# Negating the imaginary query plane on ScalarE instead of VectorE, in a chunked complex linear-attention stage

## What is computed

```
c = (u @ W_qkva.T + b_qkva) as complex q, k, v, a   # 8 heads of 32
a = a * (rsqrt(|a|^2) * sigmoid(log |a|^2))
h_t = a_t * h_(t-1) + k_t (x) v_t        # (x): outer product, all complex
y_t = q_t . h_t
```

## Time and profile before

| | us |
|---|---|
| median of 3 runs | 3847.2 (3846.6 to 3855.82) |
| profiled execution, its time | 3847.57 |
| profiled execution, span of the records | 3845.7 |
| TensorE matmul busy | 2886.4 (75%) |
| VectorE busy | 2164.3 (56%) |
| ScalarE busy | 1078.8 (28%) |
| GpSimd busy | 653.4 (17%) |
| mean granted TensorE clock | 0.806 of full |
| share of the chain that ended last | PE 57%, DVE 21%, ACT 6%, POOL 5% |

### The profile page before, as it was taken

The page is one execution under the profiler, slowest core; times in us unless marked ns, Lnnn a source line. Parts: engine busy times, 40 slices in busy tenths (PEclk is TensorE's granted clock), DMA queues, the critical chain, the costliest instruction groups (busy, mean ns, idle before and its releaser), DMA issues.

```text
span 3845.7 us, 81835 instructions
## 1 busy us (share of the span) xinstructions
PE 2886.4 (75%) x35776; PEld 2163.0 (56%) x35776; DVE 2164.3 (56%) x4688; ACT 1078.8 (28%) x2076; POOL 653.4 (17%) x682
## 2 busy tenths in 40 slices
PE   4368669867986898499759866986688458999990
PEld 3244457445744664476447545744554447888880
DVE  4445776587659666956685677658544930101004
ACT  0212253124312522333243225312412322222220
POOL 0323300420060016002400420051001000000006
PEclk8577878877787878697868877887779678999995
DMA  2122201210121122012201220121100006565645
GB/s 80 23 56 51 45 2 47 71 29 17 42 71 18 40 46 55 8 40 57 45 7 40 61 45 2 51 67 24 40 23 33 2 21 215 191 193 193 200 152 175
DMA packets 230022, 247.56 MB, mean 64 GB/s; under 512 B 147360, under 2 KB 187168, under 8 KB 227360
## 3 DMA queue, kind: packets, MB, share of 16 engines
q1 hardware_dynamic: 223520, 225.54, 20.6%
q0 software_dynamic: 6144, 16.79, 1.4%
HBM read 196.15 MB, written 46.14 MB: 63 GB/s over the span
## 4 chain that ended last, share of the span: by engine, by line
PE 57%; DVE 21%; ACT 6%; POOL 5%; issue 4%; DMA 1%; SPq 0%; POOLq 0%; DVEq 0%
PE banks L1814 13%; PE banks L2316 7%; PE banks L2335 7%; PE banks L2047 4%; PE banks L2113 3%; POOL arena L1706 3%; PE banks L2128 2%; PE banks L1824 2%; PE banks L2133 2%; PE banks L1941 2%; POOL arena L1750 2%; PE banks L1946 2%; PE banks L1951 1%; PE banks L2069 1%; DVE arena L1468 1%
## 5 line engine op out<-in xcount | busy, mean ns | idle before, releaser
L1706 POOL TENSOR_TENSOR arena<-arena 128x1 f32<-128x1 f32 (+30 forms) x496 | 435.6, 909 | 607.1 <-DMA arena<-n_d 441.0
L2113 PE MATMUL banks<-arena 32*32 32x64 f32 (+2 forms) x6144 | 209.7, 327 | 215.8 <-DVE h_tok L1370 68.2
L1727 POOL DMA_INDIRECT h_d<-h_tok,pos_now x64 | 66.7, 1043 | 1707.4 <-DVE pos_now L1571 1690.3
L1149 DVE TENSOR_REDUCE arena<-arena 128x1 f32<-128x1 f32 (+30 forms) x496 | 243.7, 502 | 172.7 <-POOL arena L1706 168.3
L2113 PE MATMUL banks<-arena,xn 32*32 32x64 f32 (+2 forms) x6144 | 197.6, 330 | 181.7 <-DVE xn L1471 89.1
L2113 PEld LDWEIGHTS banks<-arena 32*32 32x32 f32 (+2 forms) x6144 | 191.4, 202 | 236.7 <-issue 144.8
L1814 PE MATMUL banks<-hT,ring 128*128 128x512 f32 x640 | 313.1, 642 | 8.7 <-DVE arena L1293 8.5
L2113 PEld LDWEIGHTS banks<-arena,xn 32*32 32x32 f32 (+2 forms) x6144 | 181.6, 198 | 196.1 <-issue 98.0
L881 ACT ACTIVATE arena<-banks 32x512 f32<-32x512 f32 x256 | 150.4, 588 | 455.0 <-DVE xn L1471 240.5
L2316 PE MATMUL banks<-arena 128*128 128x256 f32 x1248 | 276.7, 380 | 0.0
L2335 PE MATMUL banks<-arena 128*128 128x256 f32 x1248 | 275.7, 379 | 0.0
(11 more groups left out here) (337 smaller groups left out, 5247.3 us busy)
## 6 DMA issues: line engine op xcount, KB each, us to landing
arena<-in_w_ring SPq DMA_DIRECT2D x78, 1024.0 KB, 5.0
ring<-in_w_ring SPq DMA_DIRECT2D x104, 512.0 KB, 4.6
arena<-h_d SPq DMA_DIRECT2D x39, 256.0 KB, 5.3
y_d<-arena SPq DMA_DIRECT2D x39, 256.0 KB, 5.8
n_d<-NA SPq DMA_DIRECT2D x8, 1024.0 KB, 3.9
arena<-n_d SPq DMA_DIRECT2D x16, 512.0 KB, 7.5
u_d<-arena SPq DMA_DIRECT2D x8, 1024.0 KB, 3.8
NA<-u_d SPq DMA_DIRECT2D x32, 256.0 KB, 5.6
```

Of the source, the lines that this page charges most:

```text
L1149: dve.tensor_reduce(Usub[:, c, 0:t, t], part, AX.X, ALU.add).then_inc(*up(sub_sum, me))
L1706: pool.tensor_tensor(part, Usub[:, c, 0:t, 0:t], Nsub[:, c, t, 0:t].unsqueeze(1).to_broadcast([P, t, t]), ALU.mult)\
L2113: i_ = mm(bank[4 * hg + h][keys, b * width:(b + 1) * width], K2[rows_, r, b, keys], q, start=(r == 0), stop=(r == 1), skip_group_check=True)
```

## The change

ScalarE makes the negated plane everywhere, and VectorE no longer does. A semaphore `q_neg` marks the plane of the fresh queries (made by ScalarE after it has evicted them), `q_sum` is raised by VectorE's additions of the equal-token step and of every level, and `q_ready` is now raised by ScalarE, in a new function `turn_sign(k, hg)`. ScalarE's list becomes one loop over steps and groups: `turn_sign(k, hg)` first, then what the step has of `take_blocks`, or of `lay_near` and `lay_middle`. `lay_far` stays behind the loop. VectorE waits for `q_neg` ahead of line 1426 and for `q_ready` ahead of line 1454.

```diff
 # ScalarE, evicting the planes
+                            if c == 3:
+                                act.wait_ge(*at(plane_ok, n + 1))
+                                act.activation(Q3[:, 0], Q3[:, 2], ACT.Copy, scale=-1.0).then_inc(*up(q_neg, me))
 # ScalarE, steps
+                    def turn_sign(k, hg):
+
+                        act.wait_ge(*at(q_sum, 2 * k + hg + 1))
+                        Q3 = Q3s[hg]
+                        if k:
+                            halves = "p r b (n two m) -> p r (b n) two m"
+                            act.activation(Q3[:, 0:1].rearrange(halves, two=2, m=1 << (k - 1))[:, 0, :, 1],
+                                           Q3[:, 2:3].rearrange(halves, two=2, m=1 << (k - 1))[:, 0, :, 1], ACT.Copy,
+                                           scale=-1.0).then_inc(*up(q_ready, me))
+                        else:
+                            act.activation(Q3[:, 0], Q3[:, 2], ACT.Copy, scale=-1.0).then_inc(*up(q_ready, me))
...
-                    act.wait_ge(*at(q_ready, 3 * HG))
-                    act.wait_ge(*at(k_ready, HG))
-                    for k, hg in itertools.product(range(2, INNER + 1), range(HG)):
-                        take_blocks(k, hg)
-                    act.wait_ge(*at(zeroed, 6))
-                    for hg in range(HG):
-                        lay_near(hg)
-                    for hg in range(HG):
-                        lay_middle(hg)
+                    for k, hg in itertools.product(range(STEPS), range(HG)):
+                        turn_sign(k, hg)
+                        if k == 2 and hg == 0:
+                            act.wait_ge(*at(k_ready, HG))
+                        if 2 <= k <= INNER:
+                            take_blocks(k, hg)
+                        if k == INNER + 1:
+                            act.wait_ge(*at(zeroed, 6))
+                            lay_near(hg)
+                            lay_middle(hg)
                     for hg in range(HG):
                         lay_far(hg)
 # VectorE, fresh queries and equal-token step
-                        dve.wait_ge(*at(plane_ok, 6 * hg + 4))
-                        dve.tensor_scalar(Q3[:, 0], Q3[:, 2], -1.0, None, ALU.mult).then_inc(*up(q_ready, me))
...
+                        dve.wait_ge(*at(q_neg, hg + 1))
...
-                        step(dve.tensor_tensor(q2, t1[:, :, :], t2[:, :, :], ALU.add))
-                        dve.tensor_scalar(Q3[:, 0], Q3[:, 2], -1.0, None, ALU.mult).then_inc(*up(q_ready, me))
+                        dve.tensor_tensor(q2, t1[:, :, :], t2[:, :, :], ALU.add).then_inc(*up(q_sum, me))
 # VectorE, levels
+                        dve.wait_ge(*at(q_ready, 2 * lev + hg + 1))
...
-                        step(dve.tensor_tensor(q_hi, tmp(t1), tmp(t2), ALU.add))
-                        dve.tensor_scalar(q_lo[:, 0], q_hi[:, 1], -1.0, None, ALU.mult).then_inc(*up(q_ready, me))
+                        dve.tensor_tensor(q_hi, tmp(t1), tmp(t2), ALU.add).then_inc(*up(q_sum, me))
 # TensorE
-                        pe.wait_ge(*at(q_ready, 2 * k + hg + 1))
+                        pe.wait_ge(*(at(q_ready, 2 * (k - 1) + hg + 1) if k else at(q_neg, hg + 1)))
...
-                        pe.wait_ge(*at(q_ready, 2 * STEPS + hg + 1))
+                        pe.wait_ge(*at(q_ready, 2 * (STEPS - 1) + hg + 1))
```

More of the change, by code:

```diff
@@ L331, in build @@
         u_in = signal("u_in", nxt=64)
-        dve_step = signal("dve_step", rest=226, nxt=13, pre=36)
+        dve_step = signal("dve_step", rest=210, nxt=13, pre=36)
         pre_var = signal("pre_var", pre=1)
@@ L359, in build @@
         a_ok = signal("a_ok", rest=16)
-        q_ready = signal("q_ready", rest=18)
+        q_ready = signal("q_ready", rest=16)
+        q_neg = signal("q_neg", rest=2)
+        q_sum = signal("q_sum", rest=16)
         masked = signal("masked", rest=12)
@@ L987, in turn @@
                              kpT_ok, xx_ok, wt_ok, o_sq, ot_ok, exp_ok, sg_ok, u_ok, plane_ok, mag_root,
-                             hx_ok, block_ok, laid, laid_middle, y2_ok, kt_ok, y3_ok, h_tok_ok, rt_root, rt_exp])
+                             hx_ok, q_neg, q_ready, block_ok, laid, laid_middle, y2_ok, kt_ok, y3_ok, h_tok_ok, rt_root, rt_exp])
                 act.sem_inc(started.handle, 1)
@@ L1585, in turn @@
                              logit_sub, comb_ok, comb_copied, hid0_ok, x_done, mag_ok, v3_ok, a_ok,
-                             q_ready, masked, state_ok, hsq_ok, rt_var, rt_gap, hot_ok,
+                             q_sum, masked, state_ok, hsq_ok, rt_var, rt_gap, hot_ok,
                              pos_ok, k_ready])
```

## The result

| | before | after |
|---|---|---|
| median, us | 3846.9 (3842.8 to 3855.8, 4 runs) | 4086.0 (4079.6 to 4095.0, 4 runs) |
| profiled span, us | 3845.7 | 4085.1 |
| VectorE busy, us | 2164.3 | 2135.2 |
| ScalarE busy, us | 1078.8 | 1141.9 |
| mean granted TensorE clock | 0.806 | 0.788 |

The changed kernel takes 1.062 times as long (95% interval 1.0592 to 1.0647), 239 us more. VectorE does 29 us less work. Since every edit shifts lines, line 1468 of before is 1485 after, 1379 is 1397, 881 is 886, and the negation is line 898.

What follows compares the result with a forecast made beforehand. The prediction took VectorE to bound the levels and ScalarE the tail. Levels 14.3, tail 13.25 and clock 2.1 made 29.6 us a run, times 8 = 237 us on 3847.57, so 4084 us, range 4030 to 4118.

Steps and rivals of the forecast that it cites:

- The two parts: The stage: levels bound by VectorE, then a tail bound by ScalarE; predicted +14.3 and +13.25 us a run.
- Rival 1: ScalarE's block copies don't wait behind the negation, so only savings remain: 30 us faster, 3817 us; chance 0.03.
- Rival 2: Levels stall, but near and middle copies keep their lead in the tail: 114 us more, 3962 us; chance 0.05.
- rival 3: The tail loss holds but levels are cheaper, a unit costing 1.0 us: 4026 us; chance 0.06.
- Rival 4: TensorE's lower clock stays through the outputs and all that follows up to outputs(1): 4146 us; chance 0.05.
- Rival 5: No change, since the turn does not wait for the stage's end: 3847 us; chance 0.01.
- The unit: Levels 1 to 4: masked copy starts 1.92 us later in each of 8 units, 15.4 us a run.
- The savings: VectorE without negations: 0.45 us in group 1's equal-token step and 0.33 us in a unit.
- The tail: From level 5's group 0 sum to the outputs: near copies wait behind a negation, +13.25 us a run.
- The clock: TensorE idles ahead of the outputs, which then start at the lower clock: +2.1 us a run, 0 to 3.2.
- The sum: Levels, tail and clock together: 29.6 us a run, 237 us over 8 runs, giving 4084 us.

Runs made afterwards that it cites:

- waits_only: Against the kernel before: only ScalarE's list put in the new order with its waits, VectorE still making every negation; +245.3 us, ratio 1.0636.
- copies_first: Against the kernel after: block copies put ahead of the negation in steps 2 to 5, tail as changed; +99.9 us against the kernel before, ratio 1.0257.
- tail_freed: Against the kernel after: in the tail, near and middle copies reordered around the negations, levels as changed; +157.7 us against the kernel before, ratio 1.0402.
- no_negation: Against the kernel before: all query negations left out, so part of the scores uses a stale plane; -30.4 us, ratio 0.9926.
- both_freed: Against the kernel after: all block, near, middle and far copies put ahead of negations that would hold them up; -19.9 us against the kernel before, ratio 0.9951.
- late_on_vector: Against the kernel after: copies freed in the levels, negations of levels 5 and 6 on VectorE; -27.6 us against the kernel before, ratio 0.9936.
- neg_longer: Against the kernel after: three tiny ScalarE instructions added ahead of each level's negation; +267.8 us against the kernel before, ratio 1.0685.

## Why the prediction was right

**The two parts.** VectorE bound the levels, ScalarE the tail, and the order of ScalarE's list was what mattered: waits_only has the loss without the moved work, and copies_first and tail_freed give back the one part and the other. Rival 1 (copies don't wait behind the negation) is void by the 64 waits of 2.2 us. Rival 2 (only the levels) by the tail of 24.2 us, rival 3 (cheaper units) by the cost of a unit, (14.65 + 0.45 + 0.66)/8 = 1.97 us. Rival 4 (clock low through all that follows) by the outputs, which reach 0.71 us a block before they end. Rival 5 by the time itself.

**The unit.** Its masked copy was expected 2.84 us after the sum's end. It came after 2.77 in the unit shown and 2.89 in the one at 504 (503.54 + 0.69 to 507.12), which is also the median of all 64. The term that was sized slightly wrong is the negation: 0.36 us until the copies follow, measured 0.34 in the first such unit of each run of the stage and 0.44 in most of the others (504.26 to 504.70). The levels rose by 14.65 us where 14.3 stood.

**The savings.** 0.45 for the equal-token step and 0.33 for each of 10 units, 3.75 us: the levels without any negation are 3.72 us shorter (75.85 to 72.13). That group 0's earlier start would be lost at TensorE also held: the equal-token sums wait for it 21.3 us over the span, 16.3 before.

**The tail.** +13.25 expected, +13.45 measured, with the order near, middle, near, middle and both last sums waiting for TensorE (16 waits, 67.5 us).

**The clock.** +2.1 expected, +2.79 measured. TensorE by stretch of 1 to 4 us: busy time, granted clock, DMA:

```profile
566.00:570.00 4.00, 3.56 (x64) 0.59 0.02 4
570.00:573.00 3.00, 0.00 (x0) 0.95 0.00 0
573.00:574.00 1.00, 0.84 (x4) 0.50 0.00 0
578.00:579.00 1.00, 1.00 (x8) 0.50 0.00 0
580.00:581.00 1.00, 1.00 (x13) 1.00 0.00 0
```

And the same outputs in order of time:

```profile
573.16 1.19 PE L2144 MATMUL banks<-arena 128*128 128x128 f32 x4 [3.60 <-ACT arena L859]
574.28 1.13 PE L2149 MATMUL banks<-arena 128*64 128x128 f32 x8
...
579.69 0.71 PE L2144 MATMUL banks<-arena 128*128 128x128 f32 x4
```

The granted clock had risen to 1.00 by the end of group 1's scores (0.59 in the stretch that holds them, 0.95 in the next), but TensorE did nothing for 3.60 us and was back at 0.50 when the outputs started. They run at 0.50 until past 579, some 6 us, near the upper end of the 3.5 to 6.5 I had allowed; for that lower end no row had been given. Three pairs of blocks took 6.53 us (573.16 to 579.69) where three at the full clock take 3.7, and that is the 2.8 us.

So it is in every trace. Where TensorE idles for at most 0.6 us ahead of the outputs (before, tail_freed, no_negation, both_freed, late_on_vector), they start at 1.00 and take 9.9 us; where it idles for 3.5 to 3.9 us (after, waits_only, copies_first, neg_longer), they run at 0.50 from their start on (in copies_first sometimes from 0.5 us later) and take 11.5 to 12.7 on average. The direction agrees with the rule of the Trainium skill (TensorE: Matmul & The Clock Gate, Part 1) that activity is what releases the throttle. No run here changed the clock alone: the 2.8 us came and went with the gap.

**The sum.** 14.65 + 13.45 + 2.79 = 30.9 us a run, 247 in all, 10 more than forecast. The span grew by 239.4. The other 8 us are in what follows `outputs(0)`: the eight stretches from there to the next stage add up to 2615.8 us before and 2607.7 after. From turn to turn such a stretch of the kernel before differs by 5 us with the same work in it (269.6 and 264.4 us in the third and fourth), and turn by turn the kernel after is between 4.5 us shorter and 4.2 us longer, so I take this for scatter; what makes it is open. The forecast's distance of 2 us from the median is thus two misses of 8 to 10 us that cancel, and that much of its closeness is luck.

## What to carry to other kernels

When work moves to another engine, look at what stands behind the new wait in that engine's list before you price the work: here 0.1 us more for each negation would have cost little, and a wait ahead of copies that had been made early cost 31 us a segment. An engine that is only a quarter busy may be living on a lead, and the lead is visible as copies that end long before their reader, with no idle time in front of the reader. Put instructions whose inputs come early ahead of the one whose input comes last; here that took the loss of 6.2% to one of 2.6% by a single line moved, and to a gain of 0.5% with the tail treated likewise.

## What the runs showed beyond that

The kernel before took 3846.9 us in the first session and 3872.7 and 3873.7 in the two of the experiments, 0.7% more, about as much as a change of this kind may bring; only comparisons within a session could have shown the gains above. There is no trace of the kernel before from the later sessions, but outside the stage all nine kernels have the same code. In the delta rule TensorE makes small 32x32 matmuls and VectorE waits for them. That wait over the whole span, in the kernel before (first session) and then in no_negation (a later one):

```profile
DVE NA L1229 <- PE banks L1910: 48.9, 14, 10.4
```

```profile
DVE NA L1229 <- PE banks L1908: 76.6, 15, 10.6
```

In the kernel after it is 48.9 us too, and in all seven kernels of the experiments it is between 75.4 and 77.9. These 26.5 to 29 us more are about the 25.8 and 26.8 by which the kernel before was slower. TensorE's own waits in that place, in one turn, first session and then no_negation:

```profile
PE banks L1906 <- issue: 1.4, 1, 1.4
```

```profile
PE banks L1904 <- issue: 2.2, 4, 0.9
PE banks L1908 <- issue: 1.8, 3, 1.0
```

TensorE sat idle for nothing that the trace shows, once for 1.4 us in the one and in seven places for 4.0 us in the other. Why, and whether it hangs on the chip, these runs don't tell.
